# A graph layer whose scatter-add is split between gathered rows and dense counts: a pause ahead of each gather, and more dense batches

## The chip, the cores and the metric

One Trainium2 chip, one NeuronCore. The metric is the device time of one execution in microseconds (us). The kernel before takes 1590.65 us, the median of three runs (1589.46 to 1591.73).

## What is computed

The layer works on a graph of 6250 nodes with 128 features and 206250 edges; each edge has a source, a destination and one of three types, and the edges are sorted by destination. The reference, cut to what matters:

```
h = relu(layernorm(x))
for t in 0..2:
    msg_t = relu(h[src] @ W_e[t].T + b_e[t]) where edge_type == t, else 0
    agg_t = segment_sum(msg_t, dst)              # one row for each node
agg = concat(relu(h), agg_0, agg_1, agg_2)
out = x + h + (agg @ W_n[type of the node].T + b_n[type of the node])
```

All of it is float32. The inputs are random, so a message row depends only on (source, type): there are 3 x 6250 of them, fewer than edges.

## The kernel before, in words

**Prologue.** The node rows are normalised in 49 blocks of 128. For each block TensorE (PE) makes the messages of all three types, and SP writes them into a table in device memory, `message_table`, one row of 128 for each (node, type). Meanwhile VectorE turns the edge arrays into indices and keys (lines 1134 to 1194).

**Two ways to sum an edge.** The sorted edges are cut in two. The first `E0` of them are *gathered*: groups of 512 edges (`NS` = 231 groups, four tiles of 128 edges each). For each tile GpSimd (POOL) issues one indirect DMA that fetches 128 rows of the message table into the buffer `rows` (lines 643 to 650, six slots of one group each); VectorE makes a one-hot of the edges' destinations within a window of 20 nodes (`hot`, line 1202); PE multiplies both (`gathered`, line 763, eight records a group at L770), and VectorE adds the window into the accumulator `acc` (`add`, line 1299).

The last edges are *dense*: 23 batches of two windows, each of 15 tiles of 128 edges, so 3840 edges a batch. A batch isn't gathered at all. For each type in turn, VectorE makes one-hots of the source's low seven bits (`lhot`, L1230) and of the pair (source's high bits, destination's place in the window) (`jhot`, L1216); PE multiplies them into counts (`count`, line 780, L791, 46 matmuls a batch and type, in six units); ScalarE copies the counts out of PSUM (`counted`, L957); PE then multiplies the counts with the messages of all 49 blocks, held in SBUF as three bfloat16 planes (`product`, line 796, L807, 49 matmuls in seven pieces); a reduction, a transpose and an add bring the result into `acc`. With three types that is `NQ` = 69 passes over a batch, here called type-batches.

**Order of the work.** Everything after the prologue runs in numbered steps. Each step has one gathered group, and a planner (`dealt`, line 125, and `plan`, line 148) hands the 897 pieces of dense work (units and products, the first six units apart) out to steps 1 to `NS` - 7 by their sizes. As soon as a block of 128 nodes has all its edges it is closed (`finish`, line 817 on PE and 1339 on VectorE): PE multiplies it with the node weights (L825, L826, L829), VectorE adds the selected type to `x` (L1346), SP stores it and loads the next block's operands. In a step with a closing block the planner puts less dense work, which leaves one small piece in 34 of the steps. Each engine's program follows the same list of steps; an engine waits only on semaphores. PE's are `d_build` (a unit's bank is ready: ScalarE's copy and VectorE's next one-hots wait for it), `d_prod`, and `grp_mm` (a gathered group is done). GpSimd waits for `grp_mm` before it overwrites a slot, that is, for the group six before.

**Planes.** The messages of a type are split into three bfloat16 planes, seven nodes' blocks at a time (seven chunks). For type 0 this is done at the start: SP loads a chunk (`load_planes`, line 542), ScalarE and VectorE cast and subtract (lines 960 to 966 and 1321 to 1329). `SPLIT` (line 202) says at which step each chunk is split. For the other two types the planes are made on the way, parked in device memory and fetched when the type begins (`keep`, `fetch`); `kept_step` counts from the last value of `SPLIT`.

**LEAD** (line 32) is a number of extra rows ahead of the dense windows in the tile that holds their edges: `LEAD` + 2 x `BATCHES` must be a multiple of 16, at most 64. Those rows are loaded (`dense_rows`, line 501) and turned into padding (line 628).

The tile `std` [128 x 49] holds the standard deviations of the prologue; nothing reads it after `inverses` (line 1103).

Of the kernel before, what the change touches and what calls it, by code (L numbers as in the profile page):

```python
# [15 lines left out]
TPG = 4  # L16
# [8 lines left out]
PAD_SRC = 2666666  # L25
PAD_TYPE = -T * PAD_SRC

BATCHES = 23
BW = 2
WT = 15  # L30
WE = WT * P
LEAD = 2
SLOTS = 6
OFF = (0, 3, 9, 11)
WID = (8, 8, 7, 9)
# [27 lines left out]
def build(nc, x, src, dst, etype, ntype, w_e, b_e, w_n, b_n, out):  # L63
# [9 lines left out]
    TD = T * D  # L73
    NW = BATCHES * BW
    E0 = E - NW * WE
    LR = LEAD + NW
    GD = -(-E0 // GE)
# [3 lines left out]
    PIECES = len(CUT) - 1  # L81
    NQ = T * BATCHES
    NA = LEFT + NB * P + SL
# [23 lines left out]
    def group_at(s):  # L107
        return NS - 1 - s
# [31 lines left out]
    def touches(g, i):  # L140
        return SLOPE * g - SLACK - MID <= (i + 1) * P - 1 and SLOPE * g + AHEAD + WG > i * P

    def wide_touches(w, i):
        first = SLOPE / TPG * (E0 // P + w * WT)
        return first - SLACK - D_MID <= (i + 1) * P - 1 and first + AHEAD + SL > i * P


    def plan(hand):
        at = {i: s for s in range(D0, D1 + 1) for kind, i in hand[s] if kind == "prod"}
        last = [at[q * MC + MC - 1] for q in range(NQ)]  # L150
        wide_done = [last[NQ - BATCHES + w // BW] + 2 for w in range(NW)]
        ready = [max([s for s in range(NS) if touches(group_at(s), i)] + [wide_done[w] for w in range(NW) if wide_touches(w, i)])
# [46 lines left out]
        return [j for j in range(NB) if FIN[j] == s]  # L199


    SPLIT = (-1, -1, -1, 0, 0, 0, 2)

    def splits_at(s):
        return [m for m in range(MC) if SPLIT[m] == s]


    def kept_step(k):
        t, c = divmod(k, MC)
        a, z = (PROD_STEP[t * BATCHES * MC] if t else SPLIT[-1]) + 5, PROD_STEP[((t + 1) * BATCHES - 2) * MC]  # L210
        return a + (z - 6 - a) * c // (MC - 1)

    KEEP = [kept_step(k) for k in range((T - 1) * MC)]
    FETCH = [PROD_STEP[((k // MC + 1) * BATCHES - 1) * MC + k % MC] for k in range((T - 1) * MC)]

# [6 lines left out]
    with ExitStack() as ctx:  # L222
        def sb(name, shape, dt=F32):
            return ctx.enter_context(nc.sbuf_tensor(name, shape, dt))

        def sem(name):
            return ctx.enter_context(nc.semaphore(name))
# [15 lines left out]
        def far(a):  # L243
            return a[:, ES:EW]
# [38 lines left out]
        col_s = sb("col_s", [1, -(-GD // 4) * 4], I32)  # L283
        col_d = sb("col_d", [1, BATCHES, 4], I32)
        flag = sb("flag", [1, 4], I32)
# [25 lines left out]
        std = sb("std", [P, NB])  # L311
# [72 lines left out]
        tab_mm = sem("tab_mm")  # L384
        tab_msg = [sem(f"tab_msg{i}") for i in range(UN)]
        tab_out = [sem(f"tab_out{i}") for i in range(MN)]
        landed = [sem(f"landed{i}") for i in range(SLOTS)]
        hot_ok = sem("hot_ok")
        grp_mm = sem("grp_mm")
# [71 lines left out]
        def wide_keys(to, m):  # L461
            n = 2 * TPG
            b = (m - PAIR) // 2
            return (to[:, :, b * n:(b + 1) * n].rearrange("p w (c h) -> p c h w", h=2),
                    psE[m % 2][:, :].rearrange("p (c h w) -> p c h w", h=2, w=HALF)[:, :, :, LEAD:LR])

# [10 lines left out]
        def _(sp):  # L477
# [20 lines left out]
            def dense_tiles(e0):  # L498
                return e0[E0 - LEAD * WE:E].rearrange("(w u j) -> w u j", u=WT, j=P)

# [104 lines left out]
        def _(pool):  # L605
# [10 lines left out]
                      allow_small_or_imprecise_dtypes=True).then_inc(consts, 1)  # L616
            pool.iota(bound[:, SB_:GB], [[0, 1]], base=E0 // P - LEAD * WT, channel_multiplier=WT,
                      allow_small_or_imprecise_dtypes=True).then_inc(consts, 1)
# [8 lines left out]
            for h in range(2):  # L627
                pool.memset(far(e_typ)[h * HALF:h * HALF + LEAD, :], PAD_TYPE).then_inc(lead_ok, 1)
                pool.wait_ge(lead_ok, h + 1)
# [13 lines left out]
            for s in range(NS):  # L643
                if s >= SLOTS:
                    pool.wait_ge(grp_mm, s - (SLOTS - 1))
                for u in range(TPG):
                    pool.indirect_dma_start(  # L647
                        out=rows[:, s % SLOTS, u, :], out_offset=None, in_=table_rows,
                        in_offset=bass.IndirectOffsetOnAxis(ap=idx[:, group_at(s), u:u + 1], axis=0),
                    ).then_inc(landed[s % SLOTS], 16)  # L650
# [392 lines left out]
        def _(dve):  # L1043
# [194 lines left out]
            def take_low():  # L1238
                dve.wait_ge(turn_t, LOW + 1)
                got = psE[LOW % 2]  # L1240
                dve.tensor_scalar(col_s[:, 0:GD], got[0:1, 0:GD], float(LEFT), None, ALU.add)
                dve.tensor_scalar(col_d[:, :, 0:BW], got[0:1, SB_ * P + LEAD:SB_ * P + LR].rearrange("p (b k) -> p b k", k=BW),
                                  float(LEFT), None, ALU.add).then_inc(turn_d, 1)
# [224 lines left out]
```

## Time and profile before

| | |
|---|---|
| runs, median (lowest to highest) | 1590.65 us (1589.46 to 1591.73) |
| profiled execution, its span from first to last instruction | 1595.0 us (no time of its own is listed beside the span) |
| PE matmuls busy | 1392.9 us, 87% |
| VectorE (DVE) busy | 1114.8 us, 70% |
| ScalarE (ACT) busy | 584.8 us, 37% |
| GpSimd (POOL) busy | 920.6 us, 58% |
| mean granted clock of PE, as a share of 2.4 GHz | 0.927 |
| gathers (DMA_INDIRECT, L647) | 924 |

How to read it: busy is the union of an engine's instructions of that kind; PE's weight loads are a row of their own (PEld) and run beside its matmuls. L770 is line 770 of the kernel. The bracket behind an instruction is the idle time of its engine just ahead of it and what ended it; "issue" is time in which nothing that the profile shows was waited for, "remote" (in the chain "another core or an unknown queue") is a wait on a semaphore whose update the profile could not put down to an instruction.

### The profile page before, as it was taken

How to read it: one execution, taken by the hardware profiler on the slowest of the kernel's cores; microseconds unless marked ns; L12 is line 12 of the kernel's file. 1: busy time of each engine (PE TensorE's matmuls, PEld its weight loads, DVE VectorE, ACT ScalarE, POOL GpSimd, SP SyncE). 2: the span in 40 equal slices, each digit the busy share in tenths (PEclk: the TensorE clock that was granted, in tenths of full speed). 3: DMA queues.
4: the chain of work that ended last, by engine and by line, in shares of the span. 5: the costliest groups of instructions: out<-in, count | busy, mean ns of one | idle time of the engine just before them, and what ended most of it. 6: DMA issues, size and time to landing. Idle time of an engine off the chain costs nothing.

```text
span 1595.0 us, 26681 instructions
## 1 busy us (share of the span) xinstructions
PE 1392.9 (87%) x9175; PEld 946.5 (59%) x9175; DVE 1114.8 (70%) x3845; ACT 584.8 (37%) x1165; POOL 920.6 (58%) x979
## 2 busy tenths in 40 slices
PE   7867998998999988898989888988797898888898
PEld 3544665666666656566666566656565565655565
DVE  8786887777878786777777676865565566555542
ACT  6753443433443433343334333432232223222220
POOL 3376666665666665655665565665555565555552
PEclk9978999998999999999999899999998899888989
DMA  9652222122222531222222223321211121111211
GB/s 283 215 136 54 74 72 78 49 74 72 77 50 61 170 88 47 76 60 57 76 79 58 54 65 110 101 54 50 55 45 50 50 52 49 50 47 49 54 46 37
DMA packets 97259, 120.60 MB, mean 76 GB/s; under 512 B 19947, under 2 KB 77170, under 8 KB 97124
## 3 DMA queue, kind: packets, MB, share of 16 engines
q0 software_dynamic: 29568, 60.61, 15.2%
q1 hardware_dynamic: 67078, 58.03, 11.8%
q8 instruction: 75, 1.23, 0.3%
q14 instruction: 60, 0.49, 0.1%
q10 hardware_dynamic: 478, 0.23, 0.0%
HBM read 93.12 MB, written 25.68 MB: 74 GB/s over the span
## 4 chain that ended last, share of the span: by engine, by line
PE 78%; another core or an unknown queue 6%; issue 6%; DVE 6%; ACT 3%; SPq 1%; DMA 0%; DVEq 0%; ACTq 0%
PE ps L807 33%; PE ps L791 23%; PE ps L770 12%; PE ps L829 6%; ACT arena L957 2%; PE ps L826 2%; DVE arena L1216 1%; DVE lhot L1230 1%; PE ps L707 1%; PE ps L814 1%; PE ps L825 1%; DMA acc<-in_dst_dram 0%; DVE work L1323 0%; DVE stats L1088 0%
## 5 line engine op out<-in xcount | busy, mean ns | idle before, releaser
L647 POOL DMA_INDIRECT rows<-message_table,idx x924 | 893.9, 967 | 601.8 <-PE ps L770 239.9
L957 ACT CAST arena<-ps 128x490 f16<-128x490 f32 (+2 forms) x966 | 495.5, 566 | 924.3 <-PE ps L791 585.0
L807 PE MATMUL ps<-mem,arena 128*128 128x384 bf16 x3381 | 659.1, 339 | 12.7 <-DVE mem L1328 6.4
L1216 DVE TENSOR_SCALAR arena<-iota_j,jkey 128x441 bf16<-128x441 f16 (+3 forms) x1794 | 465.8, 324 | 182.8 <-PE ps L791 113.8
L791 PE MATMUL ps<-arena,lhot 128*128 128x294 bf16 (+8 forms) x2622 | 398.2, 284 | 155.4 <-ACT arena L957 78.8
L807 PEld LDWEIGHTS ps<-mem,arena 128*128 128x128 f16 x3381 | 333.6, 103 | 225.8 <-issue 48.0
L791 PEld LDWEIGHTS ps<-arena,lhot 128*128 128x128 bf16 x2622 | 218.8, 102 | 270.7 <-issue 137.8
L1230 DVE TENSOR_TENSOR lhot<-ps,lkey 128x512 bf16<-128x512 f32 (+1 forms) x412 | 297.2, 721 | 0.0
L1297 DVE TENSOR_TENSOR acc<-ps,acc 128x60 f32 (+1 forms) x369 | 80.3, 218 | 267.7 <-PE ps L770 138.0
L770 PEld LDWEIGHTS ps<-onehot,rows 128*128 128x128 f32 x1848 | 250.1, 205 | 18.0 <-issue 8.1
L770 PE MATMUL ps<-onehot,rows 128*128 128x27 f32 x1848 | 244.1, 274 | 4.6 <-DVE acc L1297 4.0
L791 PE MATMUL ps<-jmid,lmid 128*128 128x147 bf16 (+3 forms) x552 | 134.9, 245 | 8.2 <-issue 5.1
L829 PE MATMUL ps<-wnT,acc 128*128 128x384 f32 x294 | 112.3, 521 | 0.4 <-issue 0.2
L829 PEld LDWEIGHTS ps<-wnT,acc 128*128 128x128 f32 x294 | 60.6, 206 | 46.6 <-issue 10.8
L1216 DVE TENSOR_SCALAR jmid<-iota_j,jkey 128x343 bf16<-128x343 f16 x276 | 85.1, 308 | 0.0
L791 PEld LDWEIGHTS ps<-jmid,lmid 128*128 128x128 bf16 x552 | 61.1, 111 | 34.7 <-issue 7.9
L1225 DVE TENSOR_TENSOR lmid<-ps,lkey 128x128 bf16<-128x128 f32 x274 | 76.4, 279 | 0.0
L1205 DVE TENSOR_TENSOR onehot<-ps,key 128x108 f32<-128x108 f32 x231 | 59.2, 256 | 0.0
L1346 DVE SCALAR_TENSOR_TENSOR xr<-ps,mask,xr 128x128 f32<-128x128 f32 x147 | 51.0, 347 | 4.8 <-PE ps L829 1.4
L826 PE MATMUL ps<-wnT,work 128*128 128x384 f32 x98 | 43.7, 528 | 0.4 <-issue 0.4
L707 PE MATMUL ps<-weT,work 128*128 128x384 f32 x96 | 39.5, 493 | 3.4 <-ACT work L906 3.4
L1318 DVE TENSOR_REDUCE slots<-ps 128x128 f32<-128x384 f32 x69 | 37.6, 545 | 0.0
(129 smaller groups left out, 412.6 us busy)
## 6 DMA issues: line engine op xcount, KB each, us to landing
rows<-message_table,idx POOLq DMA_INDIRECT x924
work<-message_table SPq DMA_DIRECT2D x21, 448.0 KB
kept_planes<-work SPq DMA_DIRECT2D x14, 672.0 KB
mem<-kept_planes SPq DMA_DIRECT2D x14, 672.0 KB
message_table<-work SPq DMA_DIRECT2D x25, 192.0 KB, 2.1
message_table<-rows SPq DMA_DIRECT2D x24, 192.0 KB, 2.0
own_hT<-work SPq DMA_DIRECT2D x49, 64.0 KB, 1.8
work<-own_hT SPq DMA_DIRECT2D x49, 64.0 KB
```

Of the source, the lines that this page charges most:

```text
L647: pool.indirect_dma_start(out=rows[:, s % SLOTS, u, :], out_offset=None, in_=table_rows, in_offset=bass.IndirectOffsetOnAxis(ap=idx[:, gro ...
L770: m = pe.matmul(to[:, :, OFF[u]:OFF[u] + WS], rows[:, s % SLOTS, u, :], onehot[:, s % 4, u, :].rearrange("p (t w) -> p t w", t=T), start=( ...
L791: t = pe.matmul(psB[m % 3][:, HB * (a - low):HB * (z - low)], rows_hot, cols_hot[:, HB * (a - D_OFF[u]):HB * (z - D_OFF[u])], start=(u == ...
L807: m = pe.matmul(psQ[q % 2][0:BW * SL, 0:3 * D], counts[q % 2][:, c * MC + e, :], planes[:, c * MC + e, :, :].rearrange("p v d -> p (v d)") ...
L826: pe.matmul(to[:, 0:TD], hT_own[:, j % 4, :], wnT[:, 0, :], start=False, stop=False)
L829: m = pe.matmul(to[:, 0:TD], nodes[:, t, i * P:(i + 1) * P], wnT[:, 1 + t, :], start=False, stop=(t == T - 1))
L957: act.copy(counts[q % 2][:, :, a:a + n], psB[m % 3][:, 0:HB * n].rearrange("p (w h) -> p h w", w=n)).then_inc(d_count, 1)
L1205: dve.tensor_tensor(onehot[:, s % 4, :, :], iota_b, key[:, group_at(s), :].unsqueeze(2).to_broadcast(shape), ALU.is_equal).then_inc(hot_ok, 1)
L1216: dve.tensor_scalar(to, iota_j[:, 0:HB * D_WID[u]], float(t * JT), jkey[:, w, u:u + 1], ALU.add, ALU.is_equal)
L1225: dve.tensor_tensor(lmid[u][:, i // 3 % 2, :], numbers, lkey[:, w, u:u + 1].to_broadcast([P, P]), ALU.is_equal)
L1230: dve.tensor_tensor(lhot[:, at:at + n, :], numbers.unsqueeze(1).to_broadcast(full), lkey[:, w, u:u + n].unsqueeze(2).to_broadcast(full), A ...
L1297: dve.tensor_tensor(there, sums_, there, ALU.add).then_inc(acc_add, 1)
```

## The change

Three things are edited. The dense batches go from 23 to 27, which leaves 201 gathered groups for 231; `LEAD` goes from 2 to 10 (10 + 54 = 64 rows). The last chunk of planes is split at step 1, was step 2. And ahead of every gather but the first, GpSimd clears `std` with an increment of the new semaphore `paced`, and waits until that increment has arrived before it issues the gather.

```
-BATCHES = 23
+BATCHES = 27
...
-LEAD = 2
+LEAD = 10
...
-    SPLIT = (-1, -1, -1, 0, 0, 0, 2)
+    SPLIT = (-1, -1, -1, 0, 0, 0, 1)
...
+        paced = sem("paced")
...
                 for u in range(TPG):
+                    if s or u:
+                        pool.memset(std[:, :], 0.0).then_inc(paced, 1)
+                        pool.wait_ge(paced, s * TPG + u)
                     pool.indirect_dma_start(
                         out=rows[:, s % SLOTS, u, :], out_offset=None, in_=table_rows,
                         in_offset=bass.IndirectOffsetOnAxis(ap=idx[:, group_at(s), u:u + 1], axis=0),
```

With it the number of gathers is 804, of type-batches 81, of dense pieces 1053, in steps 1 to 194 but for the first six, and of closing blocks 49 as before.

## Rows read from the trace of the kernel before

**Rows 1.** The page, busy time, share of the span and instructions of each engine.

```profile
PE 1392.9 (87%) x9175; PEld 946.5 (59%) x9175; DVE 1114.8 (70%) x3845; ACT 584.8 (37%) x1165; POOL 920.6 (58%) x979
```

**Rows 2.** The page, chain of work that ended last, by engine.

```profile
PE 78%; another core or an unknown queue 6%; issue 6%; DVE 6%; ACT 3%; SPq 1%; DMA 0%; DVEq 0%; ACTq 0%
```

**Rows 3.** The gathers' line alone: duration min/median/max in ns, first and last start.

```profile
L647 POOL DMA_INDIRECT rows<-message_table,idx x924: 938/944/2772, 78.3 to 1566.5; - x185
```

**Rows 4.** Timeline, 352 to 364 us: start, duration, engine, instruction, idle before.

```profile
351.93 0.94 POOL L647 DMA_INDIRECT rows<-message_table,idx  x1 [1.43 <-remote]
...
356.02 1.03 PE L791 MATMUL ps<-arena,lhot 128*128 128x392 bf16 x8
...
360.78 0.94 POOL L647 DMA_INDIRECT rows<-message_table,idx  x1 [0.30 <-issue]
...
363.50 1.33 ACT L957 CAST arena<-ps 128x441 f16<-128x441 f32 x3 [7.30 <-remote]
363.60 1.26 DVE L1216 TENSOR_SCALAR arena<-iota_j,jkey 128x392 bf16<-128x392 f16 x5 [3.14 <-remote]
```

**Rows 5.** Timeline, 231 to 237 us, an ordinary step.

```profile
231.90 0.97 PE L770 MATMUL ps<-onehot,rows 128*128 128x27 f32 x8
...
233.70 0.99 POOL L647 DMA_INDIRECT rows<-message_table,idx  x1 [0.31 <-issue]
...
235.83 1.33 ACT L957 CAST arena<-ps 128x441 f16<-128x441 f32 x3 [3.86 <-remote]
...
236.01 0.94 POOL L647 DMA_INDIRECT rows<-message_table,idx  x1 [1.33 <-remote]
```

**Rows 6.** Windows: stretch, length, busy by engine, granted clock, DMA share; sum of 205-305, 845-875, 950-980.

```profile
150.00:1595.00 1445.00, 1282.86 (x8631) 882.09 (x8629) 1000.02 (x3454) 497.90 (x955) 842.21 (x876) 0.93 0.24 65
...
sum 160.00, PE 150.71 PEld 105.89 DVE 132.29 ACT 71.33 POOL 99.59; mean PE 50.24 PEld 35.30 DVE 44.10 ACT 23.78 POOL 33.20
...
364.00:372.00 8.00, 7.79 (x33) 5.08 (x34) 5.93 (x20) 4.15 (x8) 3.38 (x4) 0.50 0.09 22
```

**Rows 7.** Windows, counting matmuls (L791) alone: PE busy (count), clock, DMA.

```profile
205.00:305.00 100.00, 33.95 (x253) 1.00 0.25 69
845.00:875.00 30.00, 10.99 (x85) 1.00 0.22 63
950.00:980.00 30.00, 10.80 (x83) 1.00 0.20 49
```

**Rows 8.** Windows, gathered matmuls (L770) alone, same stretches.

```profile
205.00:305.00 100.00, 16.65 (x136) 1.00 0.25 69
845.00:875.00 30.00, 5.87 (x48) 1.00 0.22 63
950.00:980.00 30.00, 5.89 (x48) 1.00 0.20 49
```

**Rows 9.** Chain of waits around 300 us: start, duration on the chain, work.

```profile
300.57 0.65 PE ps L826 x2
301.21 1.94 PE ps L829 x6
...
303.89 0.85 PE ps L770 x8
```

**Rows 10.** Timeline of GpSimd, two clears of the prologue.

```profile
0.25 0.10 POOL L1457 MEMSET const-float32-0.0<- 128x1 f32 x1 [0.25 <-issue]
...
43.04 0.23 POOL L633 MEMSET acc<- 128x160 f32 x1 [0.78 <-ACT work L898]
```

**Rows 11.** The page, costliest groups: busy, mean ns of one, idle before and its releaser.

```profile
L647 POOL DMA_INDIRECT rows<-message_table,idx x924 | 893.9, 967 | 601.8 <-PE ps L770 239.9
...
L1216 DVE TENSOR_SCALAR arena<-iota_j,jkey 128x441 bf16<-128x441 f16 (+3 forms) x1794 | 465.8, 324 | 182.8 <-PE ps L791 113.8
```

## The prediction, made before the changed kernel was run

> **What bounds the kernel now.** I read the page's shares first: TensorE (PE) is busy for 87% of the span, no other engine for more than 70% [rows 1], and the chain that ended last runs through PE for 78% of the span, with 6% put down to "another core or an unknown queue" [rows 2]. On one core that name can only mean a wait whose releaser the profile did not find, so it is the thing to look for. The list of the gathers' own line gives 924 of them, from 78.3 to 1566.5 us, with a median of 944 ns [rows 3].
>
> The timeline shows what the unnamed wait is. From 351.93 to 361.72 us GpSimd issues eight gathers back to back, one every (360.78 - 351.93) / 7 = 1.26 us. PE finishes a counting unit at 357.05, yet ScalarE's copy of it starts only at 363.50 and VectorE, which waits for the same semaphore, at 363.60 [rows 4]. Both idle until about 1.8 us after the last gather of the row of eight ended; PE then waits for ScalarE. So PE's semaphore updates are held while gathers follow each other without a gap. In an ordinary step the same is seen in small: the group that frees GpSimd's slot ends on PE at 232.87, in the middle of a row of four gathers (the last ends at 234.69), but GpSimd's next gather starts at 236.01, 1.3 us after its own last one, and ScalarE, idle for 3.86 us, starts at 235.83 [rows 5]. I count 145 rows of four and 36 rows of eight in the trace. The rows of eight come where a step holds a single small piece of dense work: two slots come free close together. After each long one PE stood still for several us and then runs at half clock: from 364 to 372 us the granted clock is 0.50, the 1.2 GHz level [rows 6].
>
> **What the stalls cost.** From 150 us to the end PE is busy for 1282.9 of 1445 us at a mean clock of 0.93. In three stretches without a row of eight it is busy for 150.7 of 160 us at full clock [rows 6]. Idle at that clean rate (5.8%) would be 84 us; it is 162, so 78 are extra. The clock's missing 7% of 1445 us, counted for the 89% in which PE works, is another 90. Together 168 us hang on the long rows of gathers.
>
> **The change, part by part.**
>
> *Dense batches, +12 type-batches (81 for 69).* In the clean stretches stand 421 counting matmuls (46 a batch, so 9.15 batches) and 232 gathered ones (8 a group, 29 groups) [rows 7, 8], with two of the 49 closing blocks. A group costs 0.85 us of the chain and a closing block 0.65 + 1.94, with its bias matmul about 2.8 [rows 9]. So a batch costs (160 - 29 x 0.85 - 2 x 2.8) / 9.15 = 14.2 us, idle included. Twelve cost 12 x 14.2 = +170 us on PE, which carries the end.
>
> *Gathered groups, -30.* 30 x 0.85 = -25 us on PE. On GpSimd it takes away 120 gathers of 1.26 us, which lie beside PE. Net of both: +145 us.
>
> *The pause.* Before each of 803 gathers GpSimd clears a 128x49 tile and waits for its own semaphore. The trace has no such wait between gathers. The clear lies between a 128x1 one (0.10 us) and a 128x160 one (0.23 us) [rows 10]: 0.14 us. The round trip of the semaphore is bounded by nothing on one side (it may hide in the 0.30 us of issue time that each gather has already) and by another 0.30 on the other. So a gather comes every 1.4 to 1.7 us; I take 1.6. What is queued behind the pause is only the next gather, and PE waits for a group only if GpSimd is late: 804 x 1.6 = 1286 us, from 78 us on, is covered by PE's work; a slot holds six steps of lead. The cover is gone from 1.80 us a gather (below). The clear also uses the memory path of VectorE's work: at most 804 x 0.14 = 113 us on an engine that is 83% busy where PE is 94% [rows 6]; I take nothing, bounds nothing and a few tens of us. What it brings is the breaking up of the rows of gathers: between two of them GpSimd's queue now runs empty. That this releases PE's updates is not shown by the trace, since its shortest gap that does release them, about 1.3 us, is longer than the pause. The bounds are therefore 0 and all of the 168 us. I take all of it, since what the held updates have in common in every case that I looked at is an unbroken queue of gathers and not the amount of transfer: the core's DMA engines are at 0.24 over that stretch [rows 6].
>
> *Small holds.* Rows of four hold PE's updates too, for 3 us in the step shown [rows 5]. The clean stretches' 5.8% idle is partly that; of about 1460 us of PE work it is 85. I take a quarter, -20, with bounds 0 and -60.
>
> *Split one step sooner, LEAD 10.* With more pieces a step, the first batch's product with the last chunk of planes, which was the third piece of step 3, becomes its first, so those planes must be there sooner. One plane load moves up one place in SP's queue, past nothing (no store or load of kept planes stands in those steps); ScalarE's two casts and VectorE's two subtractions of that chunk come a step earlier, beside PE. More leading rows lengthen six edge loads by a third at a time when VectorE still does statistics. Nothing, within 3 us either way.
>
> **Sum.** 1595.0 + 145 - 168 - 20 = 1552 us of span. The median of the runs shown, 1590.65, is 4.35 below the profiled span, so I forecast 1548 us. A measurement of this kernel tells about 0.2% from no change.
>
> **A rule against it.** With VectorE busy 83% in the clean stretches, the gathers keep a mean of 967 ns against their median of 944 [rows 3, 11]. The Trainium skill (SBUF — State Buffer, "SBUF: two separate sides") says that GpSimd and VectorE share a port pair under an exclusive lock, so that an instruction of the one blocks until a fast-mode one of the other ends, and that descriptor writing is locked out too. The gathers' 967 ns do not show the second half; by the first the clear would often wait for a VectorE instruction, which is the second rival below.
>
> **Rivals.**
> - *The pause is too short or the wrong thing* (it doesn't do what it is made for): the gathers still overlap in flight, and PE's updates stay held. For: only gaps of 1.3 us are seen to release. Against: the DMA share is low. All stalls stay: 1595 + 145 = 1740 of span, 1736 us. Chance 0.15; a half cure, about 1640, has 0.10.
> - *GpSimd becomes the bound.* Place: the clear and its wait, 804 times in series. The loop gives 78 + 804 p + 28 us (before, the last gather starts 28 us ahead of the end [rows 3]), which passes 1552 at p = 1.80. If each clear waits for a whole VectorE instruction of 0.32 us (the mean of L1216 [rows 11]) on top of 1.7, p is 2.0 and the span 1714, 1710 us. By the port rule of the Trainium skill (same page) this would be the outcome. Against: in a busy VectorE the gathers show no such waits. Chance 0.12.
> - *More comes back:* the small holds caused most of the clean idle and the bursts before 150 us go as well: 1500 to 1520. Chance 0.08.
> - *Break-even:* three quarters of the stalls go, no small holds: 1740 - 126 = 1614 down to about 1588. Within 0.2% with 0.05.
>
> **How the numbers follow.** The forecast has 0.50, with a range of its own from 1520 to 1585. Faster by over 0.2%: 0.50 + 0.08 = 0.58. Within 0.2%: 0.05. Slower: 0.15 + 0.10 + 0.12 = 0.37. The range goes from 1500 to 1740: half of the cases at 1736 may lie above it and a few below.
>
> **What would show it.** Right: gathers 1.4 to 1.7 us apart, no "remote" waits of 5 us or more on ScalarE, a granted clock of 0.97 or more after 150 us, PE busy for over 92% there, a step of about 7.2 us, GpSimd waiting for PE at most groups. Wrong: ScalarE still waits 7 us while PE's unit is done (first rival), or PE waits for rows of the gathers with GpSimd never idle and gathers 1.8 us or more apart (second).

## The result: 163,381.54 us, and the profile after

The changed kernel takes 163,381.54 us (median of four runs, 163,377.73 to 163,399.43) against 1591.19 us for the kernel before on the same chip (1589.46 to 1597.01). The ratio is 102.89, with an interval of 102.52 to 103.26. The forecast was 1548 us, and no rival came anywhere near. Of one run below, e2, two of the four executions lie over 1.5% above its fastest, and there the two fast ones are compared.

The page of the changed kernel: its busy times, its chain by engine, and its costliest groups (line, engine, operation, count, busy us, mean ns | idle before and its releaser).

```profile
span 163397.6 us, 618700 instructions
PE 96782.0 (59%) x168553; PEld 46630.3 (29%) x168553; DVE 54001.1 (33%) x85052; ACT 725.4 (0%) x1480; POOL 2911.7 (2%) x3275
PE 59%; DVE 30%; issue 5%; DVEq 3%; DMA 1%; POOL 1%; ACTq 0%; ACT 0%; POOLq 0%; SPq 0%; another core or an unknown queue 0%
L867 PE MATMUL ps<-arena,rows 128*128 128x384 f32 x157976 | 95070.9, 774 | 66203.9 <-DVE arena L1418 60902.7
...
L1424 DVE TENSOR_TENSOR acc<-ps,acc 128x384 f32 x19747 | 11018.0, 558 | 97980.6 <-PE ps L867 97980.6
L1418 DVE TENSOR_TENSOR arena<-arena 128x1536 f32<-128x1536 f32 x19747 | 34731.3, 1759 | 7994.6 <-issue 7994.6
L671 POOL DMA_INDIRECT rows<-message_table,arena x1612 | 1962.4, 1217 | 158927.7 <-DVEq L1415 157335.6
...
L651 POOL DMA_INDIRECT rows<-message_table,idx x804 | 782.8, 974 | 235.0 <-issue 126.3
```

Beside [rows 1], the first thing to see is the number of matmul records: 168,553 where there were 9,175. PE isn't slow; it does another amount of work. 157,976 records stand on one line, L867, that did not run at all before. The lines with large counts (L867, L1418, L1424, L671) all belong to one block of the program, which neither my reading nor the description above treats: **the recovery**. It stands behind the last step on every engine (on VectorE from L1404 of the changed kernel) and under a condition, which the diff does not touch:

```
            dve.tensor_scalar(flag[:, 0:1], rest_row[:, :], -1.0, 1.0, ALU.mult, ALU.add).then_inc(ctl_ok, 1)
...
            rest = dve.value_load(flag[0:1, 0:1], min_val=0, max_val=1)
            with dve.If(rest > 0):
                dve.wait_ge(fb_iota, 1)
                wide = [P, TPG, TD]
                dve.memset(flat[:, :], 0.0).then_inc(fb_zero, 1)
```

In the prologue the program tests every edge for whether its destination lies in the window that its tile has in the tables (`OFF`, `WID` for gathered edges, `D_OFF`, `D_WID` for dense ones). If one doesn't, `flag` is 1, and after the normal work all edges are summed again from nothing, slowly and generally: each of the 403 groups of 512 edges is gathered and multiplied against each of the 49 blocks. 403 x 49 = 19,747 rounds, the count of L1418 and of L1424, and 8 records a round (the code issues four float32 matmuls, each shown as two) are 157,976.

The timeline of the changed kernel shows where the normal work ends and what a round is (start, duration, engine, instruction, idle before).

```profile
1532.25 2.10 PE L833 MATMUL ps<-wnT,acc 128*128 128x384 f32 x6
...
1540.40 15.98 DVE L1404 MEMSET acc<- 128x19104 f32 x1 [4.46 <-issue]
...
1565.73 2.92 PE L867 MATMUL ps<-arena,rows 128*128 128x384 f32 x4 [31.38 <-DMA rows<-message_table,arena]
...
50003.24 0.56 DVE L1424 TENSOR_TENSOR acc<-ps,acc 128x384 f32 x1 [4.56 <-PE ps L867]
50004.41 1.76 DVE L1418 TENSOR_TENSOR arena<-arena 128x1536 f32<-128x1536 f32 x1 [0.41 <-issue]
50006.22 4.35 PE L867 MATMUL ps<-arena,rows 128*128 128x384 f32 x8 [3.15 <-DVE arena L1418]
```

The last block is closed at 1534.35 us. At 1540.40 VectorE clears the whole accumulator, 19,104 elements a partition, and the recovery runs from there to 163,397.6: 161,857 us / 19,747 = 8.20 us a round in the mean. A round is a chain without overlap: 1.76 us of one-hots, then matmuls, 0.56 us of adding, small vector instructions and idle time. The matmuls take 4.35 us in the round shown and 95,070.9 / 19,747 = 4.81 us in the mean, at a mean granted clock of 0.71. PE is busy for 59% and no engine for more.

**Why the flag is set.** The dense windows are counted from where the dense edges begin, `E0`. Four batches more move `E0` by 30 groups or 15,360 edges, so each of the windows stands over other edges. Worked out from the reference's inputs, four tiles then hold edges outside their windows, 22 edges of 206,250: in one window tile 6 (9 edges at place 6, where a width of 6 ends at place 5) and tile 7 (2 edges, the same), in another tile 9 (3 edges at place -1) and tile 12 (8 edges, -1). The same count gives none for 18 to 23 batches, 11 edges for 24 to 26, and all 22 for 27 to 29.

Two readings of the normal part, 150 to 1520 us, by windows (length, busy PE, PEld, DVE, ACT, POOL with counts, clock, DMA share, GB/s), and of GpSimd in the timeline where the kernel before had its long stall [rows 4]:

```profile
150.00:1520.00 1370.00, 1319.51 (x9507) 920.32 (x9508) 1149.09 (x3902) 583.31 (x1125) 865.18 (x1521) 0.99 0.22 62
```

```profile
351.07 0.95 POOL L651 DMA_INDIRECT rows<-message_table,idx  x1 [0.27 <-POOL std L649]
352.02 0.15 POOL L649 MEMSET std<- 128x49 f32 x1
...
352.45 0.95 POOL L651 DMA_INDIRECT rows<-message_table,idx  x1 [0.27 <-POOL std L649]
```

PE is busy for 96% at a clock of 0.99 (0.93 before, [rows 6]), and gathers come every 352.45 - 351.07 = 1.38 us: 0.95 of gather, 0.15 of clear and 0.27 of idle time. The unnamed waits of ScalarE in this stretch (us in total, times, longest):

```profile
ACT arena L961 <- remote: 23.5, 19, 5.9
```

Where nothing but the normal part is looked at, most of the forecast's own signs are there: PE's share, the clock, and steps of 7.16 us (gathered matmuls start from 95.8 to 1528.6 us). Two are missed narrowly, since a gather every 1.38 us lies below 1.4 and one unnamed wait of 5.9 us above 5. Whether the signs are there for the forecast's reasons is the second question of the runs.

### The profile page after: what moved, and what is told of

Read it like the earlier page. It is cut to its first block, busy times and chain, and to the rows that moved or that the text cites. A ratio compares the mean times of both kernels' runs of the same rounds, so it can differ in the third digit from the quotient of the medians.

```text
span 163397.6 us, 618700 instructions
## 1 busy us (share of the span) xinstructions
PE 96782.0 (59%) x168553; PEld 46630.3 (29%) x168553; DVE 54001.1 (33%) x85052; ACT 725.4 (0%) x1480; POOL 2911.7 (2%) x3275
## 4 chain that ended last, share of the span: by engine, by line
PE 59%; DVE 30%; issue 5%; DVEq 3%; DMA 1%; POOL 1%; ACTq 0%; ACT 0%; POOLq 0%; SPq 0%; another core or an unknown queue 0%
PE ps L867 58%; DVE arena L1418 21%; DVE acc L1424 7%; DVE arena L1427 2%; DVEq L1417 2%; DVEq L1424 1%; POOL rows L671 1%; DMA rows<-message_table,arena 1%; DMA arena<-in_dst_dram 0%; PE ps L811 0%; DVEq L1428 0%; PE ps L795 0%; ACTq L1019 0%; PE ps L877 0%; PE ps L774 0%
## 5 line engine op out<-in xcount | busy, mean ns | idle before, releaser
L867 PE MATMUL ps<-arena,rows 128*128 128x384 f32 x157976 | 95070.9, 774 | 66203.9 <-DVE arena L1418 60902.7
L867 PEld LDWEIGHTS ps<-arena,rows 128*128 128x128 f32 x157976 | 45506.8, 301 | 115767.4 <-DVE arena L1418 77496.9
L1424 DVE TENSOR_TENSOR acc<-ps,acc 128x384 f32 x19747 | 11018.0, 558 | 97980.6 <-PE ps L867 97980.6
L1418 DVE TENSOR_TENSOR arena<-arena 128x1536 f32<-128x1536 f32 x19747 | 34731.3, 1759 | 7994.6 <-issue 7994.6
L671 POOL DMA_INDIRECT rows<-message_table,arena x1612 | 1962.4, 1217 | 158927.7 <-DVEq L1415 157335.6
L1421 DVE TENSOR_SCALAR arena<-arena 128x4 f32<-128x4 f32 x19747 | 3363.3, 170 | 686.0
L1427 DVE COPY arena<-arena 128x4 f32<-128x4 f32 x19747 | 3362.5, 170 | 685.4
```

The costliest lines, as they stand in the source:

```text
L671: pool.indirect_dma_start(out=rows[:, 0, u, :], out_offset=None, in_=table_rows, in_offset=bass.IndirectOffsetOnAxis(ap=fb_idx[:, u:u + 1] ...
L867: m = pe.matmul(psS[:, 0:TD], rows[:, 0, u, :], fb_one[:, u, :], start=(u == 0), stop=(u == TPG - 1))
L1418: dve.tensor_tensor(fb_one, fb_iw.unsqueeze(1).to_broadcast(wide), fb_key[0].unsqueeze(2).to_broadcast(wide), ALU.is_equal).then_inc(fb_ho ...
L1421: dve.tensor_scalar(fb_key[1], fb_key[0], float(TD), None, ALU.subtract)
L1424: dve.tensor_tensor(there, psS[:, 0:TD].rearrange("p (n t) -> p t n", t=T), there, ALU.add).then_inc(fb_add, 1)
L1427: dve.tensor_copy(fb_key[0], fb_key[1])
```

## The experiments

Two questions. First: is the recovery all of it, and who sets it off? Second: in the normal part, is it the pause that ends the held updates of PE, or is it the 27 batches, which leave GpSimd fewer gathers to make up in a row? (A held update is a semaphore increment of PE that arrives late.) The runs came in five groups. The first two ran on one chip, where the kernel before takes 1596 us (1591 us in front of the forecast); groups three, four and five ran on three other chips, where **the same kernel takes 1321 us**. So times are only compared within a group; the ratio is always to the kernel before of the same group.

### Group 1 (the kernel before: 1596.01 us, 1582.51 to 1598.88, 13 runs)

**e1_pause_only**: 23 batches and everything else as before, with the pause.

```
+                    if s or u:
+                        pool.memset(std[:, :], 0.0).then_inc(paced, 1)
+                        pool.wait_ge(paced, s * TPG + u)
```

> The kernel before with the pause alone (23 batches). Theory A (gathers issued without a gap hold PE's semaphore updates, the pause frees them): the 168 us of stalls and some of the small holds go, no recovery block is entered, 1385 to 1410 us, a gather every 1.38 us, granted clock above 0.97. Theory B (the gain seen before the recovery block comes from fewer gathers and more dense work, the pause does nothing): 1591 us, within 1%. Theory C (the pause, which overwrites the tile of standard deviations, is what sends the kernel into the recovery block): about 163,000 us.

Measured: 1597.03 us (1586.45 to 1606.88), ratio 1.004 (0.9995 to 1.008). The pause alone brings nothing here.

**e2_after_no_recovery**: the changed kernel with the flag held at 0. It leaves out the sums of the 22 edges outside their windows.

```
-            dve.tensor_scalar(flag[:, 0:1], rest_row[:, :], -1.0, 1.0, ALU.mult, ALU.add).then_inc(ctl_ok, 1)
+            dve.tensor_scalar(flag[:, 0:1], rest_row[:, :], 0.0, 0.0, ALU.mult, ALU.add).then_inc(ctl_ok, 1)
```

> The changed kernel with its flag held at zero, so the recovery block is never entered; what it leaves out is the summing of those edges that lie outside their windows. Theory A: the main part alone, 1535 to 1545 us. If some of the main part's time in the changed kernel's trace were borrowed from the recovery block or paid into it, it would differ from 1540 by more than 10 us.

Measured: 1537.07 us (1520.01 to 1549.62); the two that are compared take 1520.01 and 1531.03, in the mean 1525.5. Span of the profiled one 1529.2, clock 0.972.

**e3_batches_no_recovery**: the same without the pause (27 batches, `LEAD` 10, the earlier split, flag held at 0, the same 22 edges left out).

```
-                    if s or u:
-                        pool.memset(std[:, :], 0.0).then_inc(paced, 1)
-                        pool.wait_ge(paced, s * TPG + u)
```

> 27 batches, LEAD 10 and the earlier split, without the pause, the flag held at zero as in the run before (edges outside their windows are left out). Theory A: all stalls stay and 12 type-batches more are paid, 1595 + 145 - 4 = 1736 us (1720 to 1760). Theory B: the same 1540 us as with the pause.

Measured: 1515.04 us (1512.88 to 1519.28), ratio 0.952 (0.946 to 0.959); clock 0.982. Without the pause the 27 batches are about 10 us faster than the 1525.5 with it; with 1519.28 against 1520.01 us the two ranges all but touch, so the size is uncertain.

**e4_before_forced**: the kernel before with the flag held at 1. It leaves nothing out; the recovery is added.

```
+            dve.tensor_scalar(flag[:, 0:1], rest_row[:, :], 0.0, 1.0, ALU.mult, ALU.add).then_inc(ctl_ok, 1)
```

> The kernel before with its flag held at one: nothing but the recovery block is added. If that block is the whole of the changed kernel's loss, its trace gives 163,398 - 1,537 = 161,860 us for it, so 1591 + 161,860 = 163,450 us, within 100. If the block is dearer only because the pause destroyed something it uses, this run is much shorter.

Measured: 163,581.01 us (163,570.8 and 163,591.23), ratio 102.88 (101.97 to 103.79). The recovery adds 161,985 us to a kernel without any of the change, and the time lies 31 us above the range that I had expected. e2 and e4 settle from both sides that the recovery is all of the loss: with it taken away, the change takes 1520 to 1550 us; with it added, the kernel before takes 163,581. Who sets it off is answered by f2, f6 and f7 below.

For the second question, the waits of this group from 150 to 1480 us that the profile names "remote" (engine, buffer and line: us in total, times, longest). Before:

```profile
ACT arena L957 <- remote: 190.0, 50, 9.7
POOL rows L647 <- remote: 123.9, 89, 2.3
DVE acc L1297 <- remote: 78.0, 52, 3.9
DVE arena L1216 <- remote: 49.5, 19, 6.2
```

With the pause alone (e1):

```profile
ACT arena L961 <- remote: 227.0, 84, 11.2
DVE acc L1301 <- remote: 72.2, 29, 5.6
POOL std L649 <- remote: 54.1, 47, 1.5
DVE arena L1220 <- remote: 43.7, 20, 4.3
```

With the batches and no pause (e3):

```profile
ACT arena L958 <- remote: 10.8, 9, 3.0
DVE arena L1217 <- remote: 5.4, 5, 1.4
```

441 us of such waits before, 397 with the pause (the longest of ScalarE is 11.2 us, longer than the 9.7 before), 16 with the batches. The windows of the same two runs say it in PE's terms (columns as above); e1, then e3:

```profile
150.00:1500.00 1350.00, 1206.27 (x8223) 822.80 (x8222) 987.96 (x3329) 487.04 (x931) 944.37 (x1673) 0.94 0.24 66
```

```profile
150.00:1500.00 1350.00, 1312.21 (x9528) 918.39 (x9526) 1132.04 (x3906) 578.85 (x1125) 747.85 (x762) 0.99 0.22 63
```

PE is busy for 89% at 0.94 with the pause, and for 97% at 0.99 with the batches. A timeline of GpSimd in e1 shows why the pause doesn't break the rows up:

```profile
603.79 0.95 POOL L651 DMA_INDIRECT rows<-message_table,idx  x1 [0.27 <-issue]
604.85 0.14 POOL L649 MEMSET std<- 128x49 f32 x1
605.26 0.95 POOL L651 DMA_INDIRECT rows<-message_table,idx  x1 [0.27 <-issue]
606.21 0.15 POOL L649 MEMSET std<- 128x49 f32 x1
606.64 0.95 POOL L651 DMA_INDIRECT rows<-message_table,idx  x1 [0.27 <-issue]
```

It only lengthens them, and the five lines show a gather every 1.38 to 1.47 us. A group of four now takes 4 x 1.38 = 5.5 us where it took 4 x 1.26 = 5.0, on an engine that has to make a group in each step, 6.5 us in the mean (in the kernel before the gathered matmuls start from 92.5 to 1588.8 us, 231 groups); it comes late more often and catches up in longer rows. I count some 75 rows of seven or more gathers (under 0.6 us from the end of one to the start of the next, the clear included) after 150 us in e1, 36 in the kernel before and none in e3, whose steps are 7.0 us long (99.3 to 1508.2 us, 201 groups), so that GpSimd stops after every group of four.

### Group 2 (the kernel before: 1595.73 us, 1591.32 to 1609.13, 7 runs)

**f1_gap_23**: 23 batches, and in place of the pause a real one: no group is begun before the last one has landed.

```
+                if s:
+                    pool.wait_ge(landed[(s - 1) % SLOTS], 16 * TPG * ((s - 1) // SLOTS + 1))
```

> The kernel before (23 batches) where GpSimd waits, ahead of each group, until the gathers of the group before have landed: a real gap of some 1.3 us after every row of four. Theory D (long rows of gathers hold PE's semaphore updates and stall it; a pause that leaves the gathers 1.38 us apart does not break a row, fewer groups in longer steps do): no row is longer than four, the granted clock after 150 us rises from 0.93 to above 0.98, the PE gaps over 0.8 us fall from 125 to below 40 us; the time then is set by GpSimd's loop, 231 x (3.75 + 2.5) = 1444 us from 78 us on and 28 us behind it, about 1550 us (1440 to 1560). Theory E (the short steps themselves stall PE, the rows of eight are only their consequence): the stalls stay, and the time is 1590 or more.

Measured: 1765.01 us (1763.7 to 1767.74), ratio 1.105 (1.098 to 1.111), 205 us above the range of theory D. The holds all but end, as D says, but the clock doesn't rise: it is 0.92 from 150 to 1600 us, with PE now standing still for rows. The waits of f1 from 150 to 1480 us:

```profile
POOL rows L649 <- DMA rows<-message_table,idx: 446.0, 183, 5.0
PEld ps L772 <- DMA rows<-message_table,idx: 259.3, 145, 5.5
PE ps L772 <- DMA rows<-message_table,idx: 212.9, 139, 5.3
ACT arena L959 <- remote: 10.6, 11, 1.6
```

and GpSimd in its timeline, the last gather of a group and the first of the next:

```profile
500.50 0.94 POOL L649 DMA_INDIRECT rows<-message_table,idx  x1 [0.30 <-issue]
...
503.74 0.94 POOL L649 DMA_INDIRECT rows<-message_table,idx  x1 [2.30 <-DMA rows<-message_table,idx]
```

ScalarE's unnamed wait falls from 190.0 to 10.6 us, and to 12.3 us if the stretch goes on to 1740, so that it holds the same work. The list of dense work and the gathers are the same. So the same dense work, in the same order, is next to free of holds when the gathers are issued otherwise. What it is in their issue, f1 can't say, since it brings three things at once: a stop between groups, a slower pace of gathers, and with it no step shorter than a group, which is what theory E blames. E's forecast of the time (1590 us or more) is met too, though its stalls are gone. The pace: 503.74 - 500.50 = 3.24 us lie between the two gathers, where I had reckoned with 2.5 us. A group then takes 3 x 1.25 + 3.24 = 7.0 us at least, and in the mean (1752.5 - 77.8) / 231 = 7.25 (first and last start of its gathers); 231 of them are 1675, and GpSimd is the bound: PE waits for rows for 213 us.

**f2_27_wide**: 27 batches as in the change, no pause, the recovery in place, and the four windows widened so that they hold all edges. The whole function is computed.

```
-D_OFF = (0, 4, 9, 13, 17, 21, 25, 29, 33, 37, 40, 44, 48, 51, 55)
-D_WID = (9, 9, 7, 7, 7, 7, 6, 6, 6, 7, 8, 7, 8, 9, 9)
+D_OFF = (0, 4, 9, 13, 17, 21, 25, 29, 33, 36, 40, 44, 47, 51, 55)
+D_WID = (9, 9, 7, 7, 7, 7, 7, 7, 6, 8, 8, 7, 9, 9, 9)
```

> 27 batches, LEAD 10, earlier split, no pause, the recovery block in place, and the windows of four of the fifteen dense tiles made one column wider (tiles 6, 7, 9 and 12, the two last also starting one earlier). If windows 1 and 6 missing a few edges are the whole reason for the recovery block: it is not entered, and the time is that of the run without the pause and with the flag at zero, 1515 us, plus up to 15 us for the wider one-hots. If the reason is another: about 163,500 us.

Measured: 1524.51 us (1517.92 to 1528.61), ratio 0.955 (0.949 to 0.960). The recovery isn't entered, with 27 batches, `LEAD` 10 and the earlier split all in place: the windows were what set it off.

**f3_25_wide**: 25 batches, `LEAD` 14, the earlier split, tiles 9 and 12 widened as above (6 and 7 as before), no pause.

> 25 batches (216 groups), LEAD 14, earlier split, tiles 9 and 12 one wider, no pause. Theory D: 6 type-batches fewer than 27 take 6 x 13.8 = 83 us off PE and 15 more groups add 13; if long rows stay away, 1515 - 70 = 1445 us; each long row that returns costs about 5 us, so with 20 of them 1545. Theory E: stalls go with the number of short steps, which hardly differs between 23 and 27, so no clear forecast but between 1515 and 1591.

Measured: 1492.87 us (1484.72 to 1500.86), ratio 0.932 (0.926 to 0.939). On this chip it beats the kernel before by 103 us and everything else that was run. It still has holds: `ACT arena` waits 133.0 us for "remote", 54 times, between the kernel before and f2 (10.5 us). By my count 7 rows of eight are left; at the 5 us a row that the expectation gives, theory D says some 1480 us.

**f4_25_wide_gap**: f3 with the wait of f1.

> As the 25-batch kernel, with the wait for the landing of the group before. Theory D: no long rows by construction, GpSimd's loop 216 x 6.25 = 1350 + 106 = 1456 us and PE's 1445 us lie close together: 1455 to 1480 us, at or below the kernel without the gap. Theory E: the gap adds a wait and frees nothing, the kernel is slower than without it.

Measured: 1675.49 us, ratio 1.047 (1.040 to 1.053), a miss of 195 us and more: 216 groups at the 7.25 us that f1 shows are 1566, and GpSimd is the bound again.

### Group 3 (another chip; the kernel before: 1322.23 us, 1319.06 to 1325.29, 19 runs)

**g1_three_gathers**: 23 batches; after the first six groups only three of the four gathers of a group are issued. A quarter of the gathered rows is not fetched (what lies in the slot from before is used).

```
-                for u in range(TPG):
+                for u in range(TPG if s < SLOTS else TPG - 1):
...
-                pe.wait_ge(landed[s % SLOTS], 16 * TPG * (s // SLOTS + 1))
+                pe.wait_ge(landed[s % SLOTS], 16 * TPG + 16 * (TPG - 1) * (s // SLOTS))
```

> The kernel before (23 batches, no pause) with only three of the four gathers of each group after the first six groups; what it leaves out is the fetch of a quarter of the gathered rows, PE's and VectorE's work stays the same instruction for instruction. Theory D (GpSimd's gathers, issued without a real gap, hold PE's updates): a row of three ends after 3.75 us, two groups after 7.5, so most holds go: unnamed waits fall from 440 us to below 80, the granted clock rises above 0.98, and the time to 1380 to 1430 us. Theory E (the short steps stall PE by themselves): 1590 us.

Measured: 1320.85 us, ratio 0.9994 (0.9984 to 1.0005). Here there were no holds that it could have ended. It ran again in group 4 (h1) and group 5 (i1), both on chips of this sort:

> Three of four gathers in each group, as run before beside a kernel before of 1322 us. What it leaves out is the fetch of a quarter of the gathered rows. Where the kernel before takes about 1596 us here: theory D (gathers in a row hold PE's updates) says 1330 to 1430 us with the unnamed waits down from 440 us to below 80; theory E (whatever slows that chip has nothing to do with the number of gathers) says 1590. Where it takes about 1322: both say 1321.

> Three of four gathers in each group once more (a quarter of the gathered rows isn't fetched). Where the kernel before takes about 1596 us: theory D 1330 to 1430 us, unnamed waits below 80 us; theory E 1590 us. Where it takes about 1321: 1321, and nothing is learnt.

Measured: 1321.33 us, ratio 1.0001 (0.9991 to 1.0011), and 1321.61 us, 1.0001 (0.9991 to 1.001). The question that this run was to answer on the first chip stays without an answer.

**f6_27_only**: the changed kernel without the pause, windows as they are.

> 27 batches, LEAD 10 and the earlier split with the windows as they are, no pause, the recovery block in place. If edges outside the windows of dense batches 1 and 6 are what sends the changed kernel into the recovery block, it is entered here too, without any pause: about 163,400 us. If the pause's overwriting of the standard deviations were the cause: 1515 us.

Measured: 163,340.06 us (one run). The pause has no part in the recovery; with f2 and f7 this leaves the batches, which move `E0`.

**f7_lead_only**: the kernel before with `LEAD = 18`, which moves the rows of the dense tiles and not `E0`.

> The kernel before with LEAD 18 for 2, so that the tile of dense edges has its full 64 rows as in the changed kernel, all else as before. If the extra lead rows play no part in the recovery block or in the time: within 0.5% of before, some 1595 us. If a full tile of 64 rows spoils the check of the windows: about 163,500 us.

Measured: 1325.04 us (1323.76 to 1325.54), ratio 1.002 (1.001 to 1.003). `LEAD` is innocent. This trace is also the one that stands for the kernel before on this sort of chip. Its window after 150 us, and ScalarE's copies by line:

```profile
150.00:1300.00 1150.00, 1148.00 (x8467) 824.25 (x8464) 977.17 (x3396) 480.05 (x942) 852.87 (x875) 1.00 0.29 81
```

```profile
L957 ACT CAST arena<-ps 128x490 f16<-128x490 f32 (+2 forms) x966 | 483.0, 566 | 661.8 <-PE ps L791 653.5 <-issue 7.8
```

PE is busy for 99.8% at full clock, no "remote" wait is left, and gathers come one every 1.25 us in long rows: 268 from 81.32 us on with under 0.5 us between them, and up to 36 later. The copies' mean of 566 ns is that of the first chip, so ScalarE's instructions are no faster here; by the two traces the 274 us lie in waits and in the clock. The gathers don't land sooner either: from issue to landing they take 1.8 to 4.3 us with a median of 2.0 in the trace of the kernel before, and 1.8 to 4.4 with a median of 2.0 here.

**f5_27_wide_pause**: the whole change with the wider windows of f2.

> The whole change with the four dense tiles made one column wider, so that no edge is missed: pause, 27 batches, LEAD 10, earlier split, recovery block in place. Expected: the recovery block is not entered, and the time is that of the change with the flag at zero, 1537 us, plus 5 to 10 us; against the same kernel without the pause (1524.5 us) the pause costs 10 to 25 us.

Measured: 1497.91 us (1495.81 to 1499.17), ratio 1.132 (1.130 to 1.135).

### Group 4 (a third chip; the kernel before: 1320.88 us, 1319.13 to 1323.05, 13 runs)

**h2_pause_only**: the kernel of e1.

> The pause alone at 23 batches. Where the kernel before takes about 1596 us: the same time, as measured (1597). Where it takes 1322: the gathers' loop becomes 78 + 924 x 1.38 + 28 = 1381 us, above PE's 1322, if GpSimd may not fall behind; so 1365 to 1385 if the pause is in series with everything, and 1322 to 1330 if PE's work covers it.

Measured: 1405.18 us (1403.68 to 1406.32), ratio 1.063 (1.061 to 1.065). Slower by 84 us, and above both of the expected ranges. By the page of h2 (chain by engine, the two groups of GpSimd) and its waits from 150 to 1290 us:

```profile
POOL 76%; issue 18%; PE 4%; ACT 1%; DMA 1%; DVE 1%; SPq 0%; ACTq 0%; DVEq 0%; POOLq 0%
L651 POOL DMA_INDIRECT rows<-message_table,idx x924 | 902.2, 976 | 268.8 <-POOL std L649 247.6
L649 POOL MEMSET std<- 128x49 f32 x923 | 150.6, 163 | 0.8
```

```profile
PEld ps L774 <- DMA rows<-message_table,idx: 62.0, 74, 3.6
PE ps L774 <- DMA rows<-message_table,idx: 39.3, 51, 3.3
```

The clears have 0.8 us of idle time ahead of them in all: GpSimd never waits for anything but its own pause. This is the prediction's second rival, not by a longer pause but by shorter work: its gathers start from 79.9 to 1394.9 us, one every 1.42 us in the mean (1.38 but for a few that take longer), where the kernel before ends at 1321.

**h3_27_wide**: the kernel of f2.

> 27 batches with the wider windows, no pause. Where the kernel before takes about 1596 us: 1524, as measured. Where it takes 1322: PE is then busy all the time, so 12 type-batches at PE's bare price (49 x 0.1625 + 46 x 0.103 = 12.7 us, 153 in all) and 30 groups fewer (-25) give 1322 + 128 = 1450 us (1440 to 1475), and the pause's own cost beside it is 1498 less this.

Measured: 1496.07 us (1495.22 to 1496.78), ratio 1.132 (1.130 to 1.134). Above the expected range by 20 to 55 us, and the same as f5 in ratio: at 27 batches the pause costs 2 us where it cost 84 at 23, since GpSimd's 804 x 1.42 = 1142 us lie well under PE's 1496. Of the 175 us above the kernel before, some 22 are matmuls that the wider windows add: tile 12 now crosses a border between two units in each of two windows of 81 type-batches, 162 matmuls (the page of h3 has 10,249, that of e3 10,087) at 0.135 us (1121.47 / 8300 from 150 to 1290 us). That leaves 153 for the batches, groups taken off, where the expectation had 128.

**h4_22_batches**: the kernel before with 22 batches.

```
-BATCHES = 23
+BATCHES = 22
...
-LEAD = 2
+LEAD = 4
```

> 22 batches (238 full groups and a partial one), LEAD 4, no pause, windows as before. Where the kernel before takes 1322 us, PE bounds: 3 type-batches fewer (-38) and 8 groups more (+7) give 1291 us, while GpSimd's loop, 78 + 956 x 1.25 + 28 = 1301, lies as high: 1291 to 1305. Where it takes about 1596: GpSimd's share of a step rises, more holds: 1590 to 1620.

Measured: 1310.27 us (1307.47 to 1313.72), ratio 0.992 (0.990 to 0.994): faster by 0.8%, less than expected. The kernel has 238 groups in all (952 gathers), one fewer than the expectation says. The chain of its page, and GpSimd's wait ahead of its gathers from 150 to 1290 us:

```profile
PE 43%; POOL 36%; issue 12%; DVE 5%; DMA 2%; ACT 1%; SPq 0%; POOLq 0%; DVEq 0%; ACTq 0%
```

```profile
POOL rows L647 <- issue: 267.0, 876, 0.3
```

GpSimd and PE share the chain: GpSimd issues gather after gather with never more than 0.3 us of idle time between two. Fewer batches should therefore bring nothing more; none was run. On these chips 22 is the best that was. And no unnamed wait is in this trace, so on this chip even an unbroken row of all gathers holds nothing.

### Group 5 (a fourth chip; the kernel before: 1322.03 us, 1320.02 to 1324.62, 13 runs)

**i2_24_wide**: 24 batches, `LEAD` 16, the earlier split, tiles 9 and 12 widened.

> 24 batches (224 groups), LEAD 16, earlier split, dense tiles 9 and 12 one column wider, no pause. Where the kernel before takes about 1596 us: theory D, between 25 batches (1493, eight long rows) and 23 (1596, 36 long rows), 1500 to 1550 us. Where it takes 1321: PE bounds, three type-batches and the wider tiles more, 1321 + 38 - 6 + 20 = 1373 us (1360 to 1385).

Measured: 1359.98 us (1359.49 to 1361.84), ratio 1.029 (1.028 to 1.031). It lies at the lower edge of the expected range. On these chips every batch more costs: 1310, 1321, 1360 and 1496 us for 22, 23, 24 and 27 (24 in this group, the others in group 4; 24 and 27 with wider windows).

## Why the prediction was wrong

**The step that failed is the one that isn't there.** The sum gives the recovery nothing, without a reason, where it measured 161,857 us. The prediction says of each edit what it removes, adds and moves, but takes for granted that 27 batches do the same job as 23. The paragraph on dense batches prices twelve more passes and no more; the one on `LEAD` speaks of loads and of a queue. None asks whether the tables `D_OFF` and `D_WID`, hand-written and as narrow as 23 batches allow, still fit once `E0` has moved. The sentence owed was "a block of 19,747 rounds hangs on a flag; what sets it, and does the change touch that?". Price and condition could both be had blind, the condition from the inputs, the price from the code's own loops. I listed rivals for the pause and none for the data.

**The normal part came near, for half of the reasons, and that is luck.** Beside the forecast's 1552 us of span, the changed kernel has 1540 up to the clearing, and 1520 to 1550 us without the recovery (e2). The term that cures the stalls has nearly the right size and the wrong cause.
- *Dense work, net +145.* 153 on a chip without holds (h3), wider windows taken off. Near enough.
- *The pause's price, 1.6 us a gather within 1.4 to 1.7.* 1.38: a clear of 0.15 (forecast 0.14) and 0.27 of idle time that takes the place of the 0.30 before. Just below the lower bound; the mean of h2's unbroken loop, 1.42, is inside.
- *The port rule.* The clears take 174 ns in the mean in the changed kernel, 161 to 166 in e1, h2 and f5, beside a VectorE that is busy for 84% of the time (1149.09 of 1370 us). The Trainium skill (SBUF — State Buffer, "SBUF: two separate sides") lets one engine's instruction block until a fast-mode one of the other ends; waits of that length (0.32 us a clear) are not the rule here: the median of the changed kernel's clears is 154 ns, and 18 of 803 take over 300 ns, the longest 794. Whether VectorE's instructions beside them are of the kind that the page means is not shown.
- *The pause takes the 168 us of long holds and 20 of small ones.* Wrong. At 23 batches it takes nothing (e1: 1597 for 1596); the first rival of the prediction, that the pause is too short, holds for it, though not that rival's 1736 us. What I took for a break in the queue is none: 0.42 us of clear and issue between two gathers, where the gap that I had seen to release was 1.3.
- *And yet they were gone.* 27 batches do it (e3: 1515). 1596.01 + 145 - 1515.04 = 226 us came back, more than the 188 that I had counted. I saw that a step would be some 7.2 us long and wrote it among the signs of success, but didn't see what this alone may do to the catching up: a group's four gathers take 5.0 us, so a step of 7.0 leaves GpSimd 2.0 us in which it issues nothing. The steps as measured can't be what decides, since f3's are 6.49 us (96.6 to 1492.8 us, 216 groups), no shorter or longer than the 6.51 before, with 208 us of unnamed waits for 441; but the stalls themselves lengthen the steps. Where nothing stalls, 23 batches have steps of 5.31 us (f7, 95.5 to 1315.7) and 27 of 6.95 (h3, 95.7 to 1485.7). By these PE's work leaves GpSimd 0.3 us a step at 23 batches, nothing with the pause, and 2.0 at 27. This fits the order of e1, the kernel before, f3 and e3 by their rows of seven or more gathers (75, 36, 7 and none), but is argued from them and not shown by itself.
- *The net of the pause in the change* is then a loss of about 10 us on the first chip (e2 against e3), and 2 on the others (f5 against h3, across two chips). The whole change with wider windows was not run on the first chip; by e2's 1525.5 and the 9 us between e3 and f2 it would be about 1535, an estimate.
- *Split and `LEAD`, nothing within 3 us.* `LEAD` alone is +2.8 us (f7), in the bounds. The split wasn't run by itself.
- *From span to time, -4.35.* It sets the median of other executions beside the profiled one's span. In every run here a time is 1.8 to 2.2 us above its own span, so 1552 us of span are 1554.

What stays open: why PE's updates are held on the one chip and not on the others. On the first chip the holds follow the way the gathers are issued (f1 against the kernel before, with the same list of work); on the others far longer rows hold nothing (268 in f7, all 952 in h4), and the gathers land as late on both (2.0 us in the median). Which of f1's three changes ends the holds stays open too. The run with three gathers never met a chip with holds, so that more room in a step by fewer gathers, with no batch more, does the same, was not shown.

## What to carry to other kernels

Where a kernel has a guarded slow path, a change of a size or a cut is first a question on the data: read what sets the flag, see whether the hand-fitted tables behind it are counted from the number that the change moves, and price the path by its loops (here 8.2 us x 19,747) before anything else. A wait that costs an engine time on every item does not break up a row of items that is caused by that engine being late; give it less work per step, or the others more, and look whether it then really stands still (27 batches left 16 us of unnamed waits for 441, though the reason is only argued). And where the same kernel takes 1596 us on one chip and 1321 on another, the best of the sizes run isn't the same on both (25 batches on the one, 22 on the other), so a choice made to heal a stall is to be tested on a chip that has none.

## What the runs showed of the hardware that was not expected

- The same program differs by 17% between chips, 1596 us on one and 1321 us on three, with ScalarE's copies of equal length (566 ns on both), gathers that land as late (2.0 us), and the difference in PE's updates arriving late and in the clock (0.94 and 1.00 from 150 to 1300 us).
- GpSimd went on 3.24 us after the start of the last of four indirect gathers whose landing it waited for (f1), 2.3 us after that instruction had ended.
- A clear of 128x49 with a semaphore's round trip to the same engine adds 0.13 us to a gather's period of 1.25, since it stands where 0.30 us of issue time was.
